# Down-projection weight loads of two rows of 128 instead of four, and a double-buffered second layernorm, in an attention and BitLinear block on eight cores

## The chip, the cores and the metric

The kernel runs on the 8 NeuronCores of one Trainium2 chip. The batch of 16 sequences is split by sequence: each core takes 2, and the cores exchange nothing. The time is the device time in microseconds (us) of the slowest core. All numbers of the trace below are of core 3, the slowest in the profiled execution.

## The reference

One transformer layer with layernorm after each half. Shapes are x: (16, 2048, 1024), 16 heads of 64, INNER = 4096, all float32.

```python
x = _layernorm(x + attention(x, Wq, Wk, Wv, Wr))     # additive causal penalty, softmax
x = _layernorm(x + ffn(x))

def ffn(x, w_gate, w_up, w_down):      # _bitlinear: activations rounded to 8 bits per token,
    gate = silu(_bitlinear(x, w_gate)) # weights rounded to -1, 0, 1 times one scale
    up = _bitlinear(x, w_up)
    return _bitlinear(gate * up, w_down)
```

## The kernel before

The program is written out by hand: `Builder` appends every operation to a list for its engine (`Plan.add`), with the semaphore values it waits for, and each engine goes through its list strictly in order. Every DMA, loads, stores and DMA transposes alike, is issued by one engine, SyncE, from one list (`dma`, L135 to L144; `dmat` for transposes). So a DMA whose wait is not yet met holds back every DMA listed after it. `dmat` also waits until all DMAs issued so far have landed, and every later DMA waits until that transpose has landed (`dma_floor`).

For each of its two sequences a core computes attention in head pairs (`attn_pair`), then the output projection and the first layernorm (`wr_ln1`), which leaves the normalised rows in DRAM (`y1_sc`) and their 8-bit values transposed in SBUF (`XqT`), then the feed-forward part (`ffn`). The change touches only `ffn`.

`ffn` takes the 2048 tokens in four blocks (`tsb`) of 512 tokens, four tiles of 128 tokens each (`ti` 0 to 3):

- `phase_a(tsb)`: gate and up projection of the four tiles, 512 matmuls, with weights from `wgsb` and `wusb`.
- `quant(...)`: 8-bit rounding of the hidden rows on VectorE; `quant_tr` sends their transposition to `hqT`, one DMA transpose per tile. For tiles 0 and 1 it is issued at once, for tiles 2 and 3 later.
- `phase_b(tsb, half)`: down projection of two tiles (`half` 0: tiles 0 and 1; `half` 1: tiles 2 and 3). The contraction over INNER has 32 chunks of 128. They go in groups of WOC chunks; the weights of a group are one load (`load_b`) into one of the two halves of `wdsb`. A chunk is 4 matmuls (2 tiles by 2 column halves), into PSUM banks 4 to 7. The load for group `ow + 2` goes into the half that group `ow` used, and waits for the last matmul of group `ow`. With WOC = 4 there are 8 groups of 16 matmuls and 8 loads of 1 MB, 8 KB for each partition.
- The end of `phase_b`, in the text the epilogue: for each of the two tiles (`k` 0 and 1) a load of the residual from `y1_sc` into `z2`, two `stt` operations that add the scaled bank (they free the bank), ACT's Square with the sum of squares, eight small operations on single columns of `st`, a normalising `ts` in place, and a store of `z2` to `y_out`.

The order of the blocks is written in the last lines of `ffn`: half 1 of block `tsb - 1` is put off (`pend`) until after `phase_a` and `quant` of block `tsb`; then half 0 of block `tsb` follows. In that order each sequence has three put-off half 1 phases that come in the middle, four half 0 phases, and one last half 1 phase at the end. Before a put-off phase its first two loads are already there (`pre_b`, issued before `phase_a`). Before a half 0 phase the two first loads (`pre_b0`) are listed after the epilogue of the phase ahead, then the transposes of tiles 2 and 3, then the loads from the third on. The last phase has its first two loads listed directly before it.

In the kernel before there is one `z2` buffer. So the residual load for tile `k` = 1 waits for the store of tile `k` = 0 to land.

Of the kernel before, what the change touches and what calls it, by code (L numbers as in the profile page):

```python
# [8 lines left out]
F32 = mybir.dt.float32  # L9
BF16 = mybir.dt.bfloat16  # L10
AF = mybir.ActivationFunctionType
ALU = mybir.AluOpType
# [86 lines left out]
class Builder:  # L99
# [802 lines left out]
    def ffn(self, s, XqT, cg_cols, cu_cols):  # L902
        c = self.c
        S, D, DC, JT, INNER = c.S, c.D, c.DC, c.JT, c.INNER
        OC, OTILE, TSB = c.OC, c.OTILE, c.TSB
        HB = TSB // 2 or 1
        NH = TSB // HB
        WOC = 4
        with ExitStack() as _es:
            al = lambda *a, **k: _es.enter_context(self.sbg(*a, **k)).ap()  # L910
            htsb = al("htsb", [128, TSB * INNER], F32)
# [3 lines left out]
            wusb = al("wusb", [128, 2 * DC * 512], BF16)  # L915
            wdsb = al("wdsb", [128, 2 * WOC * D], BF16)
            gts = al("gts", [128, 2 * 512], F32)
            z2 = al("z2", [128, D], F32)
            cdc = al("cdc", [128, 2 * TSB], F32)
            st = al("stat2", [128, 16], F32)  # L920
            micol_d, t_mid = self.invsw["d"]

            state = dict(
                t_g_use=[None, None], t_u_use=[None, None],
                t_d_use=[None, None], t_y_use=[None],
                gts_user=[None, None],
                t_hq_free=[None, None],
                t_hqT_use=[None] * TSB,
                t_h_free=[None] * TSB,
                t_cd_use=[None] * (2 * TSB),  # L930
                prev_apply2=None, prev_y2_store=None, prev_ms2=None,
                prev_qtok=None)

            def load_a(ot):
# [110 lines left out]
            def load_b(ow):  # L1045
                b = ow % 2
                return self.dma(
                    wdsb[:, b * WOC * D:(b + 1) * WOC * D],
                    self.wT_sc["d"][:, ow * WOC * D:(ow + 1) * WOC * D],
                    waits=[state["t_d_use"][b]])  # L1050

            def phase_b(tsb, half, pre_ld=None):
                cdo = (tsb % 2) * TSB
                tis = range(half * HB, (half + 1) * HB)
                t_dn_grp = {ti: [None] * JT for ti in tis}
                t_hqT_tp = {ti: state["t_hqT_use"][ti] for ti in tis}
                for ow in range(OC // WOC):
                    b = ow % 2
                    if pre_ld is not None and ow < len(pre_ld):
                        t_ld = pre_ld[ow]  # L1060
                    else:
                        t_ld = load_b(ow)
                    for oi in range(WOC):
                        oc = ow * WOC + oi
                        for k, ti in enumerate(tis):
                            for jt in range(JT):
                                bk = 4 + k * JT + jt
                                w0 = [t_ld, t_hqT_tp[ti]]
                                if oc == 0:
                                    w0.append(self.bank_user[bk])  # L1070
                                lastmm = (k == HB - 1 and jt == JT - 1)
                                wmm = w0 if oc == 0 else (
                                    [t_ld] if (oi == 0 and k == 0 and jt == 0)
                                    else ())
                                t_dn_grp[ti][jt] = self.mm(
                                    self.bank[bk],
                                    hqT[:, ti * OC * 128 + oc * 128:
                                        ti * OC * 128 + oc * 128 + 128],
                                    wdsb[:, b * WOC * D + oi * D + jt * 512:
                                         b * WOC * D + oi * D + jt * 512 + 512],  # L1080
                                    oc == 0, oc == OC - 1,
                                    waits=wmm,
                                    force_inc=(lastmm and oi == WOC - 1))
                    state["t_d_use"][b] = t_dn_grp[tis[-1] if False else list(tis)[-1]][JT - 1]
                for k, ti in enumerate(tis):
                    state["t_hqT_use"][ti] = t_dn_grp[ti][JT - 1]
                    tc = tsb * TSB + ti
                    t_yl = self.dma(z2, self.y1_sc[:, tc * D:(tc + 1) * D],
                                    waits=[state["t_y_use"][0],
                                           state["prev_apply2"],  # L1090
                                           state["prev_y2_store"]])
                    t_zs = []
                    for jt in range(JT):
                        bk = 4 + k * JT + jt
                        t_z = self.stt(z2[:, jt * 512:(jt + 1) * 512],
                                       self.bank[bk],
                                       cdc[:, cdo + ti:cdo + ti + 1],
                                       z2[:, jt * 512: jt * 512 + 512],
                                       ALU.mult, ALU.add,
                                       accum_out=st[:, 4 + jt:5 + jt],  # L1100
                                       waits=[t_dn_grp[ti][jt], t_yl,
                                              state["t_cd_use"][cdo + ti],
                                              state["prev_apply2"]])
                        self.bank_user[bk] = t_z
                        t_zs.append(t_z)
                    state["t_y_use"][0] = t_zs[-1]
                    if JT > 1:
                        t_sum = self.tt(st[:, 6:7], st[:, 4:5], st[:, 5:6],
                                        ALU.add, waits=t_zs)
                    else:  # L1110
                        t_sum = self.copy(st[:, 6:7], st[:, 4:5], waits=t_zs)
                    t_sq = self.act(gts[:, 0:min(D, 1024)], z2, AF.Square,
                                    accum_out=st[:, 7:8],
                                    waits=t_zs + [state["prev_ms2"],
                                                  state["gts_user"][0],
                                                  state["gts_user"][1]])
                    state["gts_user"][0] = state["gts_user"][1] = t_sq
                    t_mean = self.ts(st[:, 8:9], st[:, 6:7], 1.0 / D, None,
                                     ALU.mult, waits=[t_sum])
                    t_ms = self.ts(st[:, 9:10], st[:, 7:8], 1.0 / D, None,  # L1120
                                   ALU.mult, waits=[t_sq])
                    state["prev_ms2"] = t_ms
                    t_m2 = self.ts(st[:, 10:11], st[:, 8:9], st[:, 8:9], None,
                                   ALU.mult, waits=[t_mean])
                    t_var = self.tt(st[:, 11:12], st[:, 9:10], st[:, 10:11],
                                    ALU.subtract, waits=[t_ms, t_m2])
                    t_sd = self.act(st[:, 12:13], st[:, 11:12], AF.Sqrt,
                                    bias=self.epsc, waits=[t_var])
                    t_rs = self.recip(st[:, 13:14], st[:, 12:13],
                                      waits=[t_sd, state["prev_apply2"]])  # L1130
                    t_lb = self.stt(st[:, 14:15], st[:, 8:9], -1.0,
                                    st[:, 13:14], ALU.mult, ALU.mult,
                                    waits=[t_rs, state["prev_apply2"]])
                    t_y2 = self.ts(z2, z2, st[:, 13:14], st[:, 14:15],
                                   ALU.mult, ALU.add, waits=[t_lb, t_sq])
                    state["prev_apply2"] = t_y2
                    state["prev_y2_store"] = self.dma(
                        self.y_out[s, tc * 128:(tc + 1) * 128, :], z2,
                        waits=[t_y2])

            pend = None
            pre = None
            for tsb in range(c.NTSB):
# [5 lines left out]
                if pend is not None:  # L1149
# [5 lines left out]
                       if tsb + 1 < c.NTSB else None)  # L1155
                pend = (tsb, 1)
            phase_b(*pend, pre_ld=[load_b(0), load_b(1)])

def _make_aux():
# [39 lines left out]
```

How the kernel before makes its waits and increments, by code:

```python
                def body(eng):  # L77
                    last = {}
                    for emit, waits, inc, tag in plans.ops[eng_name]:
                        for s, v in waits:
                            if last.get(s, -1) >= v:
                                continue
                            eng.wait_ge(plans.sems[s], v)
                            last[s] = v
                        try:
                            instr = emit(eng) if emit is not None else None
                        except Exception:
                            print(f"EMIT FAILED at {tag} on {eng_name}")
                            raise
                        if inc is not None:
                            s, k = inc
                            instr.then_inc(plans.sems[s], k)
```

## Time and profile before

| what | us |
|---|---|
| median of the 2 runs shown | 7968.22 |
| the two runs | 7871.26 and 8065.18 |
| the profiled execution's own time | 7871.26 |
| its span on core 3 | 7869.7 |
| spans of the other cores in it | 7811.2 to 7856.9 |

The profiled execution is the lower of the two runs. The page of the profile gives per engine the busy time and its share of the span, then the costliest groups of instructions by line of the kernel. Since every operation goes through a helper, a line names a helper (L160 is `mm`, L171 `act`, L193 `stt`, L143 `dma`), and what tells operations apart are the tiles: `wdsb,hqT` is the down projection, `z` is the tile `z2`. "Landing" is the time from the issue of a DMA to the moment its completion is seen. "Granted clock" is the share of TensorE's full clock that it was given.

### The profile page before, as it was taken

How to read it: one execution, taken by the hardware profiler on the slowest of the kernel's cores; microseconds unless marked ns; L12 is line 12 of the kernel's file. 1: busy time of each engine (PE TensorE's matmuls, PEld its weight loads, DVE VectorE, ACT ScalarE, POOL GpSimd, SP SyncE). 2: the span in 40 equal slices, each digit the busy share in tenths (PEclk: the TensorE clock that was granted, in tenths of full speed). 3: DMA queues.
4: the chain of work that ended last, by engine and by line, in shares of the span. 5: the costliest groups of instructions: out<-in, count | busy, mean ns of one | idle time of the engine just before them, and what ended most of it. 6: DMA issues, size and time to landing. Idle time of an engine off the chain costs nothing.

```text
span 7869.7 us, 55675 instructions; the slowest of 8 cores (7811.2 to 7869.7 us)
## 1 busy us (share of the span) xinstructions
PE 5225.1 (66%) x17938; PEld 1907.1 (24%) x17938; DVE 2866.3 (36%) x4730; ACT 1126.9 (14%) x2132; POOL 0.2 (0%) x4
## 2 busy tenths in 40 slices
PE   1677767767776547765733887788778845675675
PEld 0222222222221213322311222222222212232231
DVE  1545545545544223313321443344343422322221
ACT  0112112212112001110100221122112200110010
POOL 0000000000000000000000000000000000000000
PEclk9888888888877778887866898888888877887876
DMA  4324314224322234454442000000000022445444
GB/s 99 97 59 106 84 61 107 72 66 114 73 48 55 58 79 142 142 167 138 147 166 61 11 13 16 17 11 13 17 17 6 11 83 64 131 150 171 144 122 161
DMA packets 780411, 649.70 MB, mean 83 GB/s; under 512 B 515680, under 2 KB 712544, under 8 KB 763744
## 3 DMA queue, kind: packets, MB, share of 16 engines
q1 hardware_dynamic: 780128, 646.15, 29.2%
q8 instruction: 150, 2.46, 0.1%
q14 instruction: 133, 1.09, 0.0%
HBM read 469.89 MB, written 75.50 MB: 69 GB/s over the span
## 4 chain that ended last, share of the span: by engine, by line
PE 53%; DVE 18%; DMA 17%; issue 6%; ACT 5%; SPq 1%; DVEq 0%; ACTq 0%
PE bank L160 52%; DMA wdsb<-wdT_sc 4%; ACT abuf L171 3%; DVE rls L209 3%; DMA hqT<-hq 2%; DMA otl_b<-otl_sc 2%; DMA XT_lo<-xlo 1%; DMA XT_hi<-xhi 1%; DVE khp L198 1%; DVE klp L193 1%; DVE stat L204 1%; DVE khl L198 1%; DMA z<-y_sc 1%; DVE pacc L204 1%; DVE apwl L193 1%
## 5 line engine op out<-in xcount | busy, mean ns | idle before, releaser
L171 ACT ACTIVATE abuf<-bank,negC 128x512 f32<-128x512 f32 (+3 forms) x1664 | 832.9, 601 | 3297.2 <-DVE bank L188 2475.0
L160 PE MATMUL bank<-abuf,vp 128*65 128x512 f32 x2560 | 1272.4, 657 | 0.0
L160 PE MATMUL bank<-XT_hi,apwh 128*128 128x512 bf16 x1536 | 500.5, 492 | 853.6 <-DVE apwl L193 673.9
L160 PE MATMUL bank<-wdsb,hqT 128*128 128x512 bf16 x2048 | 529.9, 422 | 579.3 <-DMA wdsb<-wdT_sc 578.9
L160 PE MATMUL bank<-klp,khl 128*128 128x512 bf16 x1280 | 511.0, 399 | 336.9 <-ACT abuf L171 313.7
L209 DVE RECIPROCAL rls<-bank 1x512 f32<-1x512 f32 x128 | 429.5, 3355 | 732.7 <-PE bank L160 732.4
L160 PE MATMUL bank<-wgsb,XqT 128*128 128x512 bf16 x2048 | 508.8, 393 | 255.7 <-DMA wgsb<-wgT_sc 254.1
L160 PEld LDWEIGHTS bank<-abuf,vp 128*65 128x65 f32 x2560 | 379.2, 153 | 856.4 <-issue 855.4
L160 PE MATMUL bank<-qlo,khp 128*128 128x512 bf16 x1280 | 514.5, 402 | 0.0
L160 PE MATMUL bank<-wusb,XqT 128*128 128x512 bf16 x2048 | 501.6, 389 | 2.6 <-DMA wusb<-wuT_sc 2.6
L188 DVE TENSOR_TENSOR htsb<-bank,gts 128x512 f32<-128x512 f32 x256 | 177.1, 692 | 885.5 <-PE bank L160 757.2
L160 PEld LDWEIGHTS bank<-XT_hi,apwh 128*128 128x128 bf16 x1536 | 178.3, 120 | 1180.7 <-issue 1113.6
L160 PE MATMUL bank<-wrh,oth_b 128*128 128x512 bf16 x512 | 181.5, 532 | 420.6 <-DMA otl_b<-otl_sc 353.0
L160 PEld LDWEIGHTS bank<-wdsb,hqT 128*128 128x128 bf16 x2048 | 212.0, 106 | 896.2 <-issue 748.0
L160 PE MATMUL bank<-XT_hi,apwl 128*128 128x512 bf16 x1536 | 349.3, 381 | 0.0
L160 PE MATMUL bank<-XT_lo,apwh 128*128 128x512 bf16 x1536 | 348.7, 380 | 0.0
L160 PEld LDWEIGHTS bank<-wgsb,XqT 128*128 128x128 bf16 x2048 | 205.0, 100 | 517.3 <-issue 313.9
L160 PEld LDWEIGHTS bank<-klp,khl 128*128 128x128 bf16 x1280 | 125.8, 98 | 819.6 <-issue 794.6
L193 DVE SCALAR_TENSOR_TENSOR z<-bank,cdc,z 128x512 f32<-128x512 f32 x64 | 45.5, 749 | 744.3 <-PE bank L160 621.1
L171 ACT ACTIVATE gts<-bank,cg_cols 128x512 f32<-128x512 f32 x256 | 176.0, 687 | 709.8 <-PE bank L160 709.7
L160 PEld LDWEIGHTS bank<-wusb,XqT 128*128 128x128 bf16 x2048 | 204.3, 100 | 260.0 <-issue 52.6
L188 DVE TENSOR_TENSOR bank<-bank,mask 128x128 f32<-128x128 f32 x512 | 139.9, 297 | 255.7 <-PE bank L160 250.9
(84 smaller groups left out, 3351.1 us busy)
## 6 DMA issues: line engine op xcount, KB each, us to landing
wdsb<-wdT_sc SPq DMA_DIRECT2D x128, 1024.0 KB, 5.3
wgsb<-wgT_sc SPq DMA_DIRECT2D x64, 1024.0 KB, 8.7
wusb<-wuT_sc SPq DMA_DIRECT2D x64, 1024.0 KB, 11.1
pw<-Wg SPq DMA_DIRECT2D x64, 512.0 KB, 4.6
pw<-Wu SPq DMA_DIRECT2D x64, 512.0 KB, 4.5
pw<-Wd SPq DMA_DIRECT2D x64, 512.0 KB, 4.9
x_tm<-x SPq DMA_DIRECT2D x2, 8192.0 KB, 27.3
xrd<-x SPq DMA_DIRECT2D x32, 512.0 KB, 5.2
```

The costliest lines, as they stand in the source:

```text
L160: e.matmul(o, l, r, start=a, stop=b),
L171: e.activation(o, i, f, bias=b, scale=s, accum_out=a),
L188: e.tensor_tensor(o, a, b, p), waits, ("dve", 1))
L193: e.scalar_tensor_tensor(o, a, s, b, p0, p1, accum_out=ac),
L198: lambda e, o=out_ap, i=in_ap: e.tensor_copy(o, i),
L204: e.tensor_reduce(o, i, AX, p, apply_absolute_value=a),
L209: lambda e, o=out_ap, i=in_ap: e.reciprocal(o, i),
```

## The change

It does two things, both in `ffn`.

1. WOC goes from 4 to 2. `wdsb` halves (16 KB to 8 KB for each partition). A `phase_b` has 16 groups of 8 matmuls and 16 loads of 512 KB (4 KB for each partition) in place of 8 groups of 16 and 8 loads of 1 MB. There are still two buffers, and `pre_b`, `pre_b0` and the loads of the last phase are still two loads. Matmuls and bytes in sum stay as they are.
2. The epilogue gets two `z2` buffers and two sets of columns in `st`, used in turn (`par`), and a scratch tile `sqb` for Square's output in place of `gts`. A buffer's residual load waits for Square, the normalising operation and the store of the tile two before. The waits on `prev_apply2`, `prev_y2_store`, `prev_ms2`, `t_y_use` and `gts_user` go from the epilogue. The order of the lists stays: load 0, operations of tile 0, store 0, load 1, operations of tile 1, store 1.

```diff
-        WOC = 4
+        WOC = 2
...
-            z2 = al("z2", [128, D], F32)
+            z2 = [al("z2a", [128, D], F32), al("z2b", [128, D], F32)]
+            sqb = al("sqb", [128, D], F32)
...
-                    t_yl = self.dma(z2, self.y1_sc[:, tc * D:(tc + 1) * D],
-                                    waits=[state["t_y_use"][0],
-                                           state["prev_apply2"],
-                                           state["prev_y2_store"]])
+                    par = state["ep_i"] % 2
+                    state["ep_i"] += 1
+                    po = 12 * par
+                    z2p = z2[par]
+                    sqp = sqb
+                    t_yl = self.dma(z2p, self.y1_sc[:, tc * D:(tc + 1) * D],
+                                    waits=state["z2_users"][par])
...
-                    t_sq = self.act(gts[:, 0:min(D, 1024)], z2, AF.Square,
-                                    accum_out=st[:, 7:8],
-                                    waits=t_zs + [state["prev_ms2"],
-                                                  state["gts_user"][0],
-                                                  state["gts_user"][1]])
-                    state["gts_user"][0] = state["gts_user"][1] = t_sq
+                    t_sq = self.act(sqp, z2p, AF.Square,
+                                    accum_out=st[:, 7 + po:8 + po],
+                                    waits=t_zs)
...
-                    state["prev_apply2"] = t_y2
-                    state["prev_y2_store"] = self.dma(
-                        self.y_out[s, tc * 128:(tc + 1) * 128, :], z2,
+                    t_st = self.dma(
+                        self.y_out[s, tc * 128:(tc + 1) * 128, :], z2p,
                         waits=[t_y2])
+                    state["z2_users"][par] = [t_sq, t_y2, t_st]
```

## Rows read from the trace of the kernel before

**Rows 1.** The page: busy time of each engine, share of the span, instructions.

```profile
PE 5225.1 (66%) x17938; PEld 1907.1 (24%) x17938; DVE 2866.3 (36%) x4730; ACT 1126.9 (14%) x2132; POOL 0.2 (0%) x4
```

**Rows 2.** The page, chain that ended last: shares of the span by engine.

```profile
PE 53%; DVE 18%; DMA 17%; issue 6%; ACT 5%; SPq 1%; DVEq 0%; ACTq 0%
```

**Rows 3.** Waits: engine, line, what for, us in total, times, longest.

```profile
PE bank L160 <- DMA wdsb<-wdT_sc: 578.9, 75, 33.3
...
DVE z L193 <- DMA z<-y_sc: 123.2, 16, 9.2
```

**Rows 4.** Chain that ended last, 7674 to 7707 us: start, duration, piece.

```profile
7674.23 4.56 DMA wdsb<-wdT_sc
7678.80 0.14 issue
7678.93 5.54 PE bank L160 x16
7684.54 4.72 DMA wdsb<-wdT_sc
```

**Rows 5.** The same chain, from the put-off phase's epilogue to the next phase.

```profile
7714.04 2.75 DMA y<-z
7716.92 3.40 DMA z<-y_sc
...
7725.89 0.34 SPq L143
7726.37 0.32 SPq L143
7726.85 7.30 DMA wdsb<-wdT_sc
...
7747.98 4.73 DMA wdsb<-wdT_sc
```

**Rows 6.** The same chain: first and last second-tile epilogue of the second sequence.

```profile
6935.20 3.23 DMA y<-z
6938.55 5.11 DMA z<-y_sc
...
7801.73 6.65 DMA wdsb<-wdT_sc
...
7853.94 3.08 DMA y<-z
7857.16 3.47 DMA z<-y_sc
```

**Rows 7.** Stretches (us, busy PE, PEld, DVE, ACT, POOL, granted clock, DMA share, GB/s): four half 0 phases.

```profile
6898.03:6928.54 30.51, 22.91 (x95) 9.51 (x96) 0.00 (x0) 0.00 (x0) 0.00 (x0) 0.85 0.60 224
...
sum 130.61, PE 98.89 PEld 39.58 DVE 0.00 ACT 0.00 POOL 0.00; mean PE 24.72 PEld 9.90 DVE 0.00 ACT 0.00 POOL 0.00
```

**Rows 8.** Stretches: sum of the three put-off phases; then the last phase.

```profile
sum 96.40, PE 73.04 PEld 29.47 DVE 37.88 ACT 0.00 POOL 0.00; mean PE 24.35 PEld 9.82 DVE 12.63 ACT 0.00 POOL 0.00
...
7801.73:7848.60 46.87, 36.13 (x128) 13.93 (x128) 0.07 (x1) 0.00 (x0) 0.00 (x0) 0.73 0.56 202
```

**Rows 9.** The page, DMA issues: number, KB each, median us to landing.

```profile
z<-y_sc SPq DMA_DIRECT2D x32, 512.0 KB, 5.5
y<-z SPq DMA_DIRECT2D x32, 512.0 KB, 3.0
```

**Rows 10.** Landing of all loads of `wdsb`, then `pw`, then `wstage`.

```profile
DMA to landing us min/median/max: 4.5/5.3/15.4
...
DMA to landing us min/median/max: 3.6/4.7/8.7
...
DMA to landing us min/median/max: 3.4/4.2/8.2
```

**Rows 11.** PE in order of time: start, duration, what, count [idle before, releaser].

```profile
7689.40 8.56 PE L160 MATMUL bank<-wdsb,hqT 128*128 128x512 bf16 x32 [0.74 <-DMA wdsb<-wdT_sc]
...
7732.00 3.57 PE L160 MATMUL bank<-wdsb,hqT 128*128 128x512 bf16 x8 [23.92 <-DMA wdsb<-wdT_sc]
```

More of the change, by code:

```diff
@@ L917, in ffn @@
             gts = al("gts", [128, 2 * 512], F32)
-            z2 = al("z2", [128, D], F32)
+            z2 = [al("z2a", [128, D], F32), al("z2b", [128, D], F32)]
+            sqb = al("sqb", [128, D], F32)
             cdc = al("cdc", [128, 2 * TSB], F32)
-            st = al("stat2", [128, 16], F32)
+            st = al("stat2", [128, 28], F32)
             micol_d, t_mid = self.invsw["d"]
@@ L924, in ffn @@
                 t_g_use=[None, None], t_u_use=[None, None],
-                t_d_use=[None, None], t_y_use=[None],
+                t_d_use=[None, None], ep_i=0,
                 gts_user=[None, None],
@@ L930, in ffn @@
                 t_cd_use=[None] * (2 * TSB),
-                prev_apply2=None, prev_y2_store=None, prev_ms2=None,
+                z2_users=[[], []],
                 prev_qtok=None)
@@ L1094, in phase_b @@
                         bk = 4 + k * JT + jt
-                        t_z = self.stt(z2[:, jt * 512:(jt + 1) * 512],
+                        t_z = self.stt(z2p[:, jt * 512:(jt + 1) * 512],
                                        self.bank[bk],
                                        cdc[:, cdo + ti:cdo + ti + 1],
-                                       z2[:, jt * 512: jt * 512 + 512],
+                                       z2p[:, jt * 512: jt * 512 + 512],
                                        ALU.mult, ALU.add,
-                                       accum_out=st[:, 4 + jt:5 + jt],
+                                       accum_out=st[:, 4 + po + jt:
+                                                    5 + po + jt],
@@ L1101, in phase_b @@
                                        waits=[t_dn_grp[ti][jt], t_yl,
-                                              state["t_cd_use"][cdo + ti],
-                                              state["prev_apply2"]])
+                                              state["t_cd_use"][cdo + ti]])
                         self.bank_user[bk] = t_z
                         t_zs.append(t_z)
-                    state["t_y_use"][0] = t_zs[-1]
                     if JT > 1:
-                        t_sum = self.tt(st[:, 6:7], st[:, 4:5], st[:, 5:6],
+                        t_sum = self.tt(st[:, 6 + po:7 + po],
+                                        st[:, 4 + po:5 + po],
+                                        st[:, 5 + po:6 + po],
@@ L1109, in phase_b @@
                                         ALU.add, waits=t_zs)
                     else:
-                        t_sum = self.copy(st[:, 6:7], st[:, 4:5], waits=t_zs)
-                    t_sq = self.act(gts[:, 0:min(D, 1024)], z2, AF.Square,
-                                    accum_out=st[:, 7:8],
-                                    waits=t_zs + [state["prev_ms2"],
-                                                  state["gts_user"][0],
-                                                  state["gts_user"][1]])
@@ L1117, in phase_b @@
-                    state["gts_user"][0] = state["gts_user"][1] = t_sq
-                    t_mean = self.ts(st[:, 8:9], st[:, 6:7], 1.0 / D, None,
+                        t_sum = self.copy(st[:, 6 + po:7 + po],
+                                          st[:, 4 + po:5 + po], waits=t_zs)
+                    t_sq = self.act(sqp, z2p, AF.Square,
+                                    accum_out=st[:, 7 + po:8 + po],
+                                    waits=t_zs)
+                    t_mean = self.ts(st[:, 8 + po:9 + po],
+                                     st[:, 6 + po:7 + po], 1.0 / D, None,
@@ L1119, in phase_b @@
                                      ALU.mult, waits=[t_sum])
-                    t_ms = self.ts(st[:, 9:10], st[:, 7:8], 1.0 / D, None,
+                    t_ms = self.ts(st[:, 9 + po:10 + po],
+                                   st[:, 7 + po:8 + po], 1.0 / D, None,
                                    ALU.mult, waits=[t_sq])
-                    state["prev_ms2"] = t_ms
-                    t_m2 = self.ts(st[:, 10:11], st[:, 8:9], st[:, 8:9], None,
+                    t_m2 = self.ts(st[:, 10 + po:11 + po],
+                                   st[:, 8 + po:9 + po],
+                                   st[:, 8 + po:9 + po], None,
@@ L1124, in phase_b @@
                                    ALU.mult, waits=[t_mean])
-                    t_var = self.tt(st[:, 11:12], st[:, 9:10], st[:, 10:11],
+                    t_var = self.tt(st[:, 11 + po:12 + po],
+                                    st[:, 9 + po:10 + po],
+                                    st[:, 10 + po:11 + po],
                                     ALU.subtract, waits=[t_ms, t_m2])
-                    t_sd = self.act(st[:, 12:13], st[:, 11:12], AF.Sqrt,
+                    t_sd = self.act(st[:, 12 + po:13 + po],
+                                    st[:, 11 + po:12 + po], AF.Sqrt,
@@ L1128, in phase_b @@
                                     bias=self.epsc, waits=[t_var])
[L1129 to L1134, printed above, removed]
+                    t_rs = self.recip(st[:, 13 + po:14 + po],
+                                      st[:, 12 + po:13 + po], waits=[t_sd])
@@ L1135, in phase_b @@
+                    t_lb = self.stt(st[:, 14 + po:15 + po],
+                                    st[:, 8 + po:9 + po], -1.0,
+                                    st[:, 13 + po:14 + po],
+                                    ALU.mult, ALU.mult, waits=[t_rs])
+                    t_y2 = self.ts(z2p, z2p, st[:, 13 + po:14 + po],
+                                   st[:, 14 + po:15 + po],
                                    ALU.mult, ALU.add, waits=[t_lb, t_sq])
-                    state["prev_apply2"] = t_y2
```

## The prediction

> **What bounds the kernel now.** I read the page first: TensorE (PE) is busy for 66% of the span and no other engine for more than 36% [rows 1]. The chain that ended last gives 53% to PE and 17% to DMA [rows 2], so there is DMA time on the path that sets the end, and the change can only matter there. The waits say where. PE waited 578.9 us for loads of `wdsb`, and VectorE (DVE) 123.2 us, 16 times, for the residual load of `z2` [rows 3]. Sixteen is the number of `phase_b` calls (2 sequences by 8): one wait in each epilogue, that of tile `k` = 1. The change touches both waits.
>
> The chain in order of time shows the first of them closely [rows 4]. In a `phase_b` PE runs 16 matmuls, then a load of `wdsb` is issued, 4.72 us later it has landed, and only then does PE go on. The reader should see load and matmuls alternate on the chain: a load is not hidden. The reason is in the code. With two buffers, the load for group `ow + 2` is issued when group `ow` ends, and all that covers it is the matmuls of group `ow + 1`. So two groups take L + G + 0.2 us, where L is a load's landing, G the time of one group's matmuls, and 0.2 the two hand-overs (0.14 after a landing and about 0.06 before an issue [rows 4]). This holds as long as L is longer than G.
>
> G comes from the stretches. From the landing of the transposes to the last matmul, the four half 0 phases of the second sequence take 130.61 us with 98.89 us of PE busy, the three put-off ones 96.40 with 73.04 [rows 7, 8]. Each holds 6 groups, so G = (98.89 + 73.04) / 42 = 4.1 us. L has a minimum of 4.5 and a median of 5.3 over all loads [rows 10]; I use 5.0 for the steady part of a phase, between the 4.72 of [rows 4] and that median. The model then gives, for the six groups of such a stretch, 4.7 (first load) + 0.14 + 2 x 4.1 + 2 x (5.0 + 4.1 + 0.2) = 31.6 us. Measured are 130.61 / 4 = 32.7 and 96.40 / 3 = 32.1. It is good to 3%, so I trust its form.
>
> **The change, part by part: smaller loads.** The same bytes now go in 16 loads of 512 KB, and a group is 8 matmuls, G' = 4.1 / 2 = 2.05 us. What decides is L', the landing of a 512 KB load. If landing were proportional to size, nothing would change. It is not. Two loads of 1 MB issued together are both there after some 7.8 us (7726.37 to 7734.15), where one alone takes 4.5 to 4.7 [rows 5, 10]; the second megabyte adds only about 3. Taking half of that off a minimum of 4.5 gives 3.0 to 3.2. Other loads of exactly 512 KB say more: `pw` never lands before 3.6 us and has a median of 4.7, `wstage` 3.4 and 4.2 [rows 10]. The nearest row is the residual load, 4 KB for each partition from a DRAM tensor with the same row pitch of 64 KB as the down weights. Alone in the queue, as in the second tile of an epilogue, it took 3.40 to about 5.3 us, on average 4.3 over the eight of the second sequence, of which the first and the last took 5.11 and 3.47 [rows 5, 6]. The lower bound is 3.0, what the median store takes [rows 9] and what the halved increment gives; the upper bound 4.7, no gain from the smaller size. I take 3.8: the floor of 3.4 plus the 0.4 to 0.5 by which the 1 MB load's steady value lies over its own floor.
>
> The Trainium skill, "DMA: Bandwidth & Descriptors", section "Anatomy of one DMA", fits a DMA as about 2.0 us fixed plus its bytes at 436 GB/s, and its rules for kernel authors ask for 1 MiB or more in one DMA. By it a 1 MB load takes 4.4 us, which the trace bears out with 4.5, and a 512 KB load 3.2 (an estimate from that fit); the residual loads here take more. With 3.2 the sum below would come out 68 us lower, at about 7923.
>
> Two groups now take 3.8 + 2.05 + 0.2 = 6.05 us, so what were two groups before takes 12.1 us in place of 9.3.
>
> - *Half 0 phases (8 in all).* After the transposes 14 groups remain in place of 6, because the two preloaded groups are half as big: 3.8 + 0.14 + 2 x 2.05 + 6 x 6.05 = 44.3 us, against 32.7: +11.6. Ahead of the transposes something is won: `pre_b0` needs 7.30 us to land, and the transposes wait for that [rows 5]. With half the bytes I take 2.5 us off. Net +9.1, times 8 = +73 us.
> - *Put-off phases (6).* 44.3 against 32.1: +12.2, times 6 = +73. The preloading in front of `phase_a` is hidden either way.
> - *Last phases (2).* 46.87 us before [rows 8]. After: 4.2 for the first load (6.65 before, two being issued together [rows 6]) + 0.14 + 4.1 + 7 x 6.05 = 50.8: +3.9, times 2 = +8.
>
> Sum: +154 us. It depends on L' with 7 loads in 14 phases and 8 in two, 114 in all: 11.4 us for each 0.1 us of L'.
>
> **The epilogue.** The residual load of the second tile waited for the store of the first to land: 2.75 us, then 3.40 us for the load, then the `stt` operations [rows 5]. In the second sequence the eight stores took 3.16 us on average, the first and last 3.23 and 3.08 [rows 6]. With two buffers the load goes out behind the store's issue, 0.48 us later (two issues in a row start 0.48 apart [rows 5]). The list order still keeps it behind the store, and the store behind the normalising operation of tile 0, so no more than the landing is won: 3.2 + 0.1 - 0.5 = 2.8 us. The load now shares the 16 DMA engines with the store's 512 KB; half of the 3 us that a further megabyte costs is 1.5 us if all of it falls into the load and nothing if the store is through. I take 0.6, so 2.2 us an epilogue. All of it is on the path, since everything that comes next (`pre_b0`, the loads of `phase_a`, the end of the sequence) is listed behind the second store. 16 x 2.2 = -35 us; the bounds are 16 x 1.3 = -21 and 16 x 2.8 = -45. The residual load of tile 0 was covered by a load (about 4.7) and a group (4.1) and now by 3.8 + 2.05 + 0.14 = 6.0 us, while its median landing over all 32 is 5.5 [rows 9]: just covered, and if the cover is gone it costs up to 1 us in each phase, +16 us. The other edits cost nothing: Square writes elsewhere but takes its place in ACT's list as before, ACT idles there, and the dropped waits had been met by earlier work of the same engine. The eight more loads and semaphore increments in a phase cost SyncE's queue 0.32 us each [rows 5], and it stands idle between loads.
>
> **Sum.** +154 - 35 = +119 us. Against the profiled execution's 7871 us that is 7990 us, 1.5% more. The median of the two runs shown, 7968, lies between the profiled run and one 2.5% above it; I reckon from the profiled one.
>
> **The rivals.**
>
> 1. *The small load lands no faster than the residual load does* (L' of 4.3 or more). For it speak the residual rows, the median of `pw`, and that the number of rows in a transfer (128) does not change; against it that the floors of all 512 KB loads are near 3.5. At 4.3: 119 + 57 = +176, 8047 us; at 4.7: +222, 8093. This is slower by over 2% from L' = 4.15 on.
> 2. *The clock falls.* PE would idle 1.95 of 6.05 us, about a third, where it now idles about a quarter of the stretch, at a granted clock of 0.73 to 0.87 [rows 7, 8]. Should it sink to 1.2 GHz, the lower of its two levels, a group of 8 would take the 3.57 us that 8 matmuls need after a wait of 23.92 us today [rows 11], and two groups 3.8 + 3.57 + 0.2 = 7.57: 1.52 more, 98 times (6 pairs in 14 phases, 7 in two), and 2 x 1.52 more at the head of 16 phases: 149 + 49 = +198 us on top, 8188. It decides (over 2% slower) once a fifth of these groups run so. Against it speaks that 32 matmuls after a gap of 0.74 us take 8.56 us [rows 11], 2.14 for 8 of them, so a short gap leaves the clock up; one of 2 us no row shows.
> 3. *The epilogue wins and the loads cost little* (L' of 3.0 or less, as for stores): 119 - 91 = +28 at 3.0, and at 2.6 -18 with a full 2.8 us an epilogue making it about -28, 7843 us: a shade faster. Break-even is at L' = 2.75. Against it: no 512 KB load of the trace landed under 3.4 in any of the rows read.
> 4. *The load size does not matter at all*, because a phase is bound by what stands ahead of it (transposes, quantisation). Then only the epilogue counts: -35, 7836 us. The alternating chain of rows 4 speaks against it.
>
> **How the numbers follow.** My forecast (L' from 3.3 to 4.15, +60 to +157) has 0.57. Rival 1 has 0.20, rival 2 has 0.08, rival 3 has 0.11, rival 4 has 0.04. The time of the likeliest is 7990 us; the range goes from 7900 (L' = 3.0) to 8110 (L' = 4.7 and a little less from the epilogue), which leaves out rivals 2 and 4 and the ends of 1 and 3. About 2% is what a measurement of this kernel can tell from no change. Over 2% slower starts at 8029 us: rivals 1 and 2 and the upper edge of the forecast, 0.32. Over 2% faster is not reached by any sum here, 0.03. The rest is 0.65.
>
> **What would show it.** In the profile after: `wdsb` landings of 512 KB with a median near 4 and a steady value near 3.8; PE's wait for `wdsb` up by about 150 us from 578.9; on the chain, 8 matmuls of about 2 us alternating with loads; the half 0 and put-off stretches at 44 us; VectorE's 16 waits for `z2`'s load shorter, and the second load's issue half a microsecond behind the store's. I am wrong if these stretches stay near 32 us, if `wdsb` lands in under 3.2 us, or if the granted clock in them drops well under 0.7.

## The result and the profile after

| | before | after |
|---|---|---|
| median of all executions, us | 8028.95 (12) | 8210.1 (13) |
| lowest, us | 7829.57 | 7993.72 |
| the profiled execution, us | 7871.26 | 7993.72 |
| ratio after to before | | 1.0202, 95% interval 1.0161 to 1.0243 |

The two medians mix in executions in which one die (four cores) or both were granted a lower clock; the ratio leaves these out, and so do the cores read below and the "quiet dies", those with a granted clock of 0.82 or more, each taken with the median time of its four cores. The 13 quiet dies of the kernel after lie at 7965 to 7985 us, median 7971; those of the kernel before, 46 over all the runs of this case, at 7801 to 7848, median 7814. So the change makes the kernel about 2% slower, some 156 us.

The profiled execution came out at 7993.72 us, where 7990 was forecast. That is luck: the forecast added too little to a base that was too high, as the part on the prediction shows. The median of 8210 lies outside the forecast range of 7900 to 8110.

First the waits of the kernel after (engine, line, what for, us, times, longest), to be held against [rows 3]:

```profile
PE bank L160 <- DMA wdsb<-wdT_sc: 744.5, 216, 32.8
...
DVE z2a L193 <- DMA z2a<-y_sc: 328.0, 6, 73.5
...
DVE z2b L193 <- DMA z2b<-y_sc: 94.1, 16, 7.7
```

PE waits for `wdsb` 216 times, not 75, and 165.6 us longer in sum. In both kernels 24 of these waits are the long ones in front of a phase and behind the transposes, 10.5 us or more each: 521 us of the 578.9 before and 530 of the 744.5 after. The short ones inside the stretches went from 59 us to 214: that is where the change costs. The second tile's wait for its residual load has fallen from 123.2 to 94.1 us, no more. The 328.0 us against `z2a` need care. They are the whole idle time of VectorE in front of six operations whose last releaser was the load; most of it is the phase itself. In only one of the 16 phases did the first `stt` start after the last matmul's end, by 0.97 us.

The DMA issues of the page after (number, KB each, median us to landing), against [rows 9, 10]:

```profile
wdsb<-wdT_sc SPq DMA_DIRECT2D x256, 512.0 KB, 3.7
```

Half the bytes land in 3.7 us where all of them took 5.3. The chain that ended last, in a put-off phase of the kernel after (start, duration, piece), answers to [rows 4, 5]:

```profile
7465.92 4.19 DMA wdsb<-wdT_sc
7470.11 0.14 issue
7470.25 5.12 PE bank L160 x16
...
7475.43 4.32 DMA wdsb<-wdT_sc
...
7479.89 1.90 PE bank L160 x8
...
7481.85 3.40 DMA wdsb<-wdT_sc
...
7485.39 1.90 PE bank L160 x8
...
7499.29 3.55 DMA wdsb<-wdT_sc
...
7502.98 1.90 PE bank L160 x8
...
7505.47 5.91 DMA z2a<-y_sc
...
7518.10 0.34 SPq L143
...
7518.58 4.51 DMA z2b<-y_sc
```

From 7475.43 to 7505.0 there are five turns of load and 8 matmuls, 5.9 us each: four such half-size groups in 11.8 us, where two groups of 16 took 9.3 on average in the half 0 and put-off phases of the kernel before. The last two lines show the new epilogue: the second residual load starts 0.48 us behind the first store's issue, as forecast, but still 0.48 us behind, and not beside the first tile's work.

The stretches from the first load after the transposes to the last matmul (us, busy PE, PEld, DVE, ACT, POOL, granted clock, DMA share, GB/s) sum over all half 0 phases of both sequences, eight of them, as follows. First the kernel before:

```profile
sum 268.50, PE 198.46 PEld 78.65 DVE 3.50 ACT 0.00 POOL 0.00; mean PE 24.81 PEld 9.83 DVE 0.44 ACT 0.00 POOL 0.00
```

And the kernel after, with the first of its eight rows:

```profile
3115.20:3160.90 45.70, 28.71 (x112) 10.58 (x112) 0.28 (x1) 0.00 (x0) 0.00 (x0) 0.90 0.56 173
...
sum 370.80, PE 233.15 PEld 85.61 DVE 3.25 ACT 0.00 POOL 0.00; mean PE 29.14 PEld 10.70 DVE 0.41 ACT 0.00 POOL 0.00
```

That is 33.6 us a phase before and 46.4 after; a stretch holds 112 matmuls in place of 96, and PE idles for 17.2 us of it in place of 8.8. The granted clock in it is 0.90, above the 0.85 of [rows 7].

### The profile page after: what moved, and what is told of

Same layout as the page of the kernel before. It is cut to its first block, busy times and chain, and to the rows that moved or that the text cites. A ratio compares the mean times of both kernels' runs of the same rounds, so it can differ in the third digit from the quotient of the medians.

```text
span 7992.2 us, 56145 instructions; the slowest of 8 cores (7952.8 to 7992.2 us)
## 1 busy us (share of the span) xinstructions
PE 5215.4 (65%) x17938; PEld 1891.2 (24%) x17938; DVE 2866.8 (36%) x4730; ACT 1127.7 (14%) x2132; POOL 0.2 (0%) x4
## 4 chain that ended last, share of the span: by engine, by line
PE 52%; DMA 18%; DVE 18%; issue 6%; ACT 4%; SPq 1%; DVEq 0%; ACTq 0%
PE bank L160 51%; DMA wdsb<-wdT_sc 6%; DVE rls L209 3%; ACT abuf L171 3%; DMA otl_b<-otl_sc 2%; DMA hqT<-hq 2%; DMA XT_lo<-xlo 1%; DMA XT_hi<-xhi 1%; DVE khp L198 1%; DVE klp L193 1%; DVE stat L204 1%; DMA z2b<-y_sc 1%; DMA pterT<-pter 1%; DVE khl L198 1%; SPq L143 1%
## 5 line engine op out<-in xcount | busy, mean ns | idle before, releaser
L160 PE MATMUL bank<-wdsb,hqT 128*128 128x512 bf16 x2048 | 538.9, 414 | 744.7 <-DMA wdsb<-wdT_sc 744.5
L193 DVE SCALAR_TENSOR_TENSOR z2a<-bank,cdc,z2a 128x512 f32<-128x512 f32 x32 | 22.8, 749 | 812.9 <-PE bank L160 484.9
```

The source lines that it names most:

```text
L160: e.matmul(o, l, r, start=a, stop=b),
L193: e.scalar_tensor_tensor(o, a, s, b, p0, p1, accum_out=ac),
```

## The experiments

Theory: the loss is a load's landing that two buffers cover with one group only. Rivals: the new epilogue costs; small loads cost in themselves. In the expectations "the changed kernel" is the kernel after. Where a profile is of another core than the slowest, its number is given.

**The load size alone.**

```diff
 (kernel before)
-        WOC = 4
+        WOC = 2
```

> The kernel before with WOC = 2 and its old epilogue. Theory (the loss is the landing of a load that two buffers cover with one group only: two groups take L' + G' + 0.2 us): the stretches from the transposes to the last matmul take 45 to 46 us as in the changed kernel, PE's wait for wdsb is about 745 us, and the time is some 28 us over the changed kernel, 1.022 to 1.026 of the kernel before. Rival (the loss comes from the new epilogue, its scratch tile, its columns or the tighter cover of its first residual load): the time stays within 0.5% of the kernel before.

Measured: 1.0245 of the kernel before, interval 1.0156 to 1.0335. PE's wait for `wdsb` and the eight half 0 stretches:

```profile
PE bank L160 <- DMA wdsb<-wdT_sc: 759.2, 213, 32.0
```

```profile
sum 372.70, PE 231.46 PEld 85.46 DVE 3.90 ACT 0.00 POOL 0.00; mean PE 28.93 PEld 10.68 DVE 0.49 ACT 0.00 POOL 0.00
```

46.6 us a stretch, as in the kernel after. Six quiet dies lie at 7984 to 8009 us, median 7992, where 15 of the kernel before on the same chip lie at 7801 to 7835, median 7810. The whole loss, and more, comes from WOC.

**The epilogue alone.**

```diff
 (kernel after)
-        WOC = 2
+        WOC = 4
...
-            sqb = al("sqb", [128, D], F32)
...
-                    sqp = sqb
+                    sqp = gts[:, 0:min(D, 1024)]
...
-                                    waits=t_zs)
+                                    waits=t_zs + [state["gts_user"][0],
+                                                  state["gts_user"][1]])
+                    state["gts_user"][0] = state["gts_user"][1] = t_sq
```

> WOC = 4 as before, with the two z2 buffers and the two column sets; Square keeps writing into gts. Theory: the stretches stay at 33 us, the 16 epilogues get about 1.8 us shorter each, and the time is 25 to 35 us under the kernel before, 0.996. Rival (the epilogue is what costs): over the kernel before by 50 us or more.

Measured: 0.9957, interval 0.9911 to 1.0003. Its eight half 0 stretches:

```profile
sum 265.20, PE 191.38 PEld 77.07 DVE 3.42 ACT 0.00 POOL 0.00; mean PE 23.92 PEld 9.63 DVE 0.43 ACT 0.00 POOL 0.00
```

The stretches stay where they were. From the last matmul to the second store's issue the 16 epilogues sum to 271 us, against 297 in the kernel before and 296 with the load size alone; in the kernel after it is 269. The epilogue part wins 1.6 to 1.8 us each time. The interval still touches 1, but the quiet dies tell the two apart: 18 of this kernel lie at 7779 to 7810 us, median 7790, some 20 us under the 7810 of the kernel before and a little less than the 25 to 35 expected. The two parts multiply to 1.0245 x 0.9957 = 1.020, the ratio of the whole change.

**Four buffers of 512 KB.** As many bytes as `wdsb` had before, but a load goes out three groups ahead of its use. `pre_b`, too, becomes four loads.

```diff
 (kernel after, Square writing into gts as above)
         WOC = 2
+        NB = 4
...
-            wdsb = al("wdsb", [128, 2 * WOC * D], BF16)
+            wdsb = al("wdsb", [128, NB * WOC * D], BF16)
...
-                t_d_use=[None, None], ep_i=0,
+                t_d_use=[None] * NB, ep_i=0,
...
-                b = ow % 2
+                b = ow % NB
...
-                pre_b0 = [load_b(0), load_b(1)]
+                pre_b0 = [load_b(i) for i in range(4)]
...
-            phase_b(*pend, pre_ld=[load_b(0), load_b(1)])
+            phase_b(*pend, pre_ld=[load_b(i) for i in range(4)])
```

> The changed kernel's loads of 512 KB, but four buffers in place of two (as many bytes of wdsb as the kernel before had), four loads issued ahead; Square keeps writing into gts. Theory (a landing of 3.7 us costs only because one group of 1.9 us covers it): with three groups (5.7 us) as cover it is hidden, the stretches fall to what PE takes, 27 to 32 us, PE's wait for wdsb drops by over 300 us, and the time is 60 to 120 us under the kernel before, 0.985 to 0.992. Rival (smaller loads cost in themselves, by the bandwidth of 4 KB rows or by SyncE's issue of twice as many): the stretches stay over 40 us and the time over the kernel before.

> Four buffers of 512 KB with the new epilogue a second time, for an interval. Theory: 0.985 to 0.992 of the kernel before. Rival: 1.00 or more.

Measured: the lowest time is 7735.57 us, with 7820.91 as the kernel before's lowest on the same chip (0.989). Neither run gave an interval. The quiet dies lie at 7703 to 7718 us in the first run (six) and 7703 to 7713 in the second (five), medians 7712 and 7709, where the kernel before has 7810 and 7813 on the two chips: 0.987 both times. The eight half 0 stretches (core 5):

```profile
3104.40:3132.00 27.60, 23.04 (x96) 9.52 (x96) 0.47 (x1) 0.00 (x0) 0.00 (x0) 0.86 0.74 248
...
sum 231.10, PE 184.77 PEld 77.23 DVE 3.33 ACT 0.00 POOL 0.00; mean PE 23.10 PEld 9.65 DVE 0.42 ACT 0.00 POOL 0.00
```

28.9 us a stretch, with the same 512 KB loads; four groups being preloaded, it holds 96 matmuls as in the kernel before, which needed 33.6. That settles the rival: small loads with deeper cover are better than large loads with shallow cover. PE's wait for `wdsb` fell less than expected, from 744.5 us to 526.0 on core 5 (expected: by over 300), since 506 us of it are the 24 long waits, which stay. The short ones fell from 214 us to 20.

**Three buffers, two loads ahead of a phase.** The same edit with `NB = 3` and `pre_b`, `pre_b0` left at two loads.

> Loads of 512 KB with three buffers, two issued ahead of a phase; Square keeps writing into gts. Theory: a load is covered by two groups, 2 x 1.9 = 3.8 us, against a landing of 3.7 plus 0.2, so the alternation all but vanishes, three groups take about 5.9 us at most, and a stretch after the transposes takes 30 to 34 us against 46 in the changed kernel. Rival (each landing grows as more loads are in flight, so that buffers win nothing): stretches of 40 us or more.

Measured on core 5:

```profile
sum 301.60, PE 223.29 PEld 87.00 DVE 3.53 ACT 0.00 POOL 0.00; mean PE 27.91 PEld 10.87 DVE 0.44 ACT 0.00 POOL 0.00
```

37.7 us a stretch of 112 matmuls: between two and four buffers, but over the 30 to 34 expected. The three quiet dies lie at 7829 to 7849 us, 7840 in the median, against 7816 for the kernel before on that chip and 7971 for the kernel after. The miss is of the landing, which I took as fixed. It grows with the loads in flight: the landings (min, median, max) with two buffers, three (core 5) and four (core 5) are

```profile
DMA to landing us min/median/max: 3.4/3.7/13.7
```

```profile
DMA to landing us min/median/max: 3.5/4.8/12.4
```

```profile
DMA to landing us min/median/max: 3.4/5.4/13.7
```

With 4.8 a turn of three groups takes 4.8 + 1.9 + 0.2 = 6.9 us, and 14 groups 14 / 3 x 6.9 + 4.9 = 37.1, close to the 37.7. This sum was made after the run. With four buffers and 5.4 a turn of four groups takes 7.5 us, just what four groups of 1.9 take on PE.

**Loads of 256 KB.** The kernel after with `WOC = 1`.

> The changed kernel with WOC = 1: 32 loads of 256 KB a phase, two buffers, groups of 4 matmuls. Theory: two groups take L'' + G'' + 0.2; with G'' = 1.0 and L'' = 3.2 (0.9 us were saved from 1 MB to 512 KB, so 0.45 for the next halving) 4.4 us, a stretch after the transposes about 67 us, the time some 340 us over the changed kernel, about 8330. Rival (landing proportional to size from here): the time stays within 50 us of the changed kernel.

> WOC = 1 a second time, since all its cores showed a low granted clock in the first run. With the landings of the first run (median 2.6 us for 256 KB, against 3.7 for 512 KB and 5.3 for 1 MB) and groups of 4 matmuls at about 1.0 us, two groups take 3.8 us; a stretch after the transposes of 30 groups 57 to 60 us; the time 8200 to 8300 us.

Measured: 8605.89 us in the first run, with all cores at a granted clock of 0.77 to 0.79, and 8329.55 in the second at 0.81 to 0.82. The first run's half 0 stretches took 67.2 us each, just what was expected, but by two errors that cancel: the landing is 2.6 us, not 3.2, and PE takes 41 us of a stretch, not the 30 of 30 groups at 1.0. So the second expectation, with the right landing, missed with its 57 to 60 us. The rows of the second run are the eight half 0 stretches, the first of them ahead of the sum, and then PE in order of time in one half 0 phase (start, duration, what, count, idle before):

```profile
3106.10:3173.50 67.40, 42.65 (x120) 11.35 (x120) 0.31 (x1) 0.00 (x0) 0.00 (x0) 0.75 0.43 125
...
sum 557.90, PE 351.34 PEld 93.94 DVE 0.73 ACT 0.00 POOL 0.00; mean PE 43.92 PEld 11.74 DVE 0.09 ACT 0.00 POOL 0.00
```

```profile
7135.43 1.74 PE L160 MATMUL bank<-wdsb,hqT 128*128 128x512 bf16 x4 [0.61 <-DMA wdsb<-wdT_sc]
7137.66 1.02 PE L160 MATMUL bank<-wdsb,hqT 128*128 128x512 bf16 x4 [0.49 <-DMA wdsb<-wdT_sc]
7140.09 3.37 PE L160 MATMUL bank<-wdsb,hqT 128*128 128x512 bf16 x8 [1.41 <-DMA wdsb<-wdT_sc]
7144.61 1.02 PE L160 MATMUL bank<-wdsb,hqT 128*128 128x512 bf16 x4 [1.15 <-DMA wdsb<-wdT_sc]
```

69.7 us a stretch. Here the second rival of the prediction does appear. A group of 4 matmuls takes 1.02 us at best, but here one takes 1.74, and 8 take 3.37 where two groups at 1.02 take 2.04; the granted clock of the first stretch is 0.75. Behind the first 32 matmuls of each phase, 211 of the 384 groups took longer than 1.07 us, and 179 of 384 in the first run. PE is busy for 351 us in place of 233, though a stretch has only 120 matmuls in place of 112. In the kernel after, most groups of 8 take 1.89 us, but not all:

```profile
7489.23 1.89 PE L160 MATMUL bank<-wdsb,hqT 128*128 128x512 bf16 x8 [1.96 <-DMA wdsb<-wdT_sc]
7491.31 1.89 PE L160 MATMUL bank<-wdsb,hqT 128*128 128x512 bf16 x8 [0.20 <-DMA wdsb<-wdT_sc]
...
7584.79 5.45 PE L160 MATMUL bank<-wdsb,hqT 128*128 128x512 bf16 x16 [2.31 <-DMA wdsb<-wdT_sc]
...
7599.72 3.50 PE L160 MATMUL bank<-wdsb,hqT 128*128 128x512 bf16 x8 [3.72 <-DMA wdsb<-wdT_sc]
```

Behind the first 32 matmuls of each phase, 9 of its 192 groups took 2.06 to 3.57 us in place of 1.89. Five of the nine come after gaps of 1.96, 1.97, 2.31, 3.72 and 3.99 us, the other four right behind a slow group. Ten other gaps of over 1.9 us were followed by a group of 1.89.

**Both residual loads ahead of the first store**, in the kernel after.

```diff
+                yls = []
+                for k, ti in enumerate(tis):
+                    tc = tsb * TSB + ti
+                    par = (state["ep_i"] + k) % 2
+                    yls.append(self.dma(z2[par],
+                                        self.y1_sc[:, tc * D:(tc + 1) * D],
+                                        waits=state["z2_users"][par]))
                 for k, ti in enumerate(tis):
...
-                    t_yl = self.dma(z2p, self.y1_sc[:, tc * D:(tc + 1) * D],
-                                    waits=state["z2_users"][par])
+                    t_yl = yls[k]
```

> The changed kernel with both residual loads of an epilogue listed one after the other, ahead of the first tile's operations and its store. Theory (the second buffer wins little because the load still stands behind the store in SyncE's list, and behind the store's bytes): the second tile's first stt starts right behind the first tile's normalising operation instead of 5 to 7 us after the store's issue, each epilogue falls from 17 to about 11.5 us, and the time is 75 to 90 us under the changed kernel. Rival (something else holds the second tile, such as ACT's Square or the banks): no more than 20 us.

The chain in one epilogue:

```profile
7218.17 0.06 DVE z2a L182
...
7218.90 1.43 DVE z2b L193 x4
...
7223.29 0.82 DVE z2b L182
```

The second tile's `stt` now follows the first tile's last operation. The 16 epilogues sum to 172 us in place of 269, so 97 us are gone from them, 6 us each. The lowest time is 7938.42 us, 55 under the lowest of the kernel after, and the six quiet dies lie at 7889 to 7923 us, median 7899, 72 under the 7971 of the kernel after; 75 to 90 were expected. Part of the gain was lost in the stretches: on cores 3, 5 and 7 of the profiled execution the eight half 0 stretches sum to 405 to 407 us, with a landing median of 4.1, where the same cores have 371 to 379 in the kernel after; on cores 0, 1 and 6 they stand at 373 to 385 (after: 370 to 377). Why loads landed later on some cores stays open.

**Four buffers and early residual loads together.**

> Four buffers of 512 KB and both residual loads ahead of the first store. Theory: the two savings add, since they lie in different stretches: about 90 us from the shorter stretches plus 75 to 90 from the epilogues and the 28 that the second buffer gives, 0.975 to 0.982 of the kernel before.

Measured: 0.9792, interval 0.9734 to 0.985, and seven quiet dies at 7611 to 7673 us, median 7614, which is 202 under the kernel before. Four buffers alone gave 98 to 104, and the 16 epilogues sum to 174 us, 97 under the 271 with four buffers alone: the two savings add.

**The next phase's loads ahead of the stores.** On top of that, `phase_b` gets a `hook`, called between the residual loads and the epilogue's operations, which lists `pre_b0` and the transposes of tiles 2 and 3, or `load_a`, or the last phase's first loads.

```diff
+                hooked = hook() if hook is not None else None
                 for k, ti in enumerate(tis):
...
+                def hook_tr():
+                    ld = [load_b(i) for i in range(4)]
+                    quant_tr(tr23)
+                    return ld
+                def hook_a(tsb=tsb):
+                    if tsb + 1 < c.NTSB:
+                        return [load_a(0), load_a(1)]
+                    return [load_b(i) for i in range(4)]
+                pre_b0 = (phase_b(*pend, pre_ld=pre_b, hook=hook_tr)
+                          if pend is not None else hook_tr())
+                pre = phase_b(tsb, 0, pre_ld=pre_b0, hook=hook_a)
```

> As the one with four buffers and early residual loads, and in addition the next phase's first loads (and the transposes of tiles 2 and 3) are listed ahead of the epilogue's stores, so that they run beside the epilogue. Theory (the epilogue costs only because the list holds the next loads behind its stores): 6 transitions to a half 0 phase win about 8 us each, 6 to phase_a about 9, 2 to the last phase about 6, together some 110 us more, 0.960 to 0.970 of the kernel before. Rival (the next phase waits for its banks or for the transposes anyway): within 40 us of the version without this reordering.

> The reordered version a second time, for an interval: its lowest time so far is 7484.5 us beside 7825.7 us for the kernel before on the same chip. Theory: 0.955 to 0.970 of the kernel before. Rival (that run was a stray low one): 0.975 or more, no better than the version without the reordering at 0.979.

> The reordered version a third time, in five rounds against the kernel before, for the interval that the two earlier runs lacked (their lowest times, 7484.5 and 7478.5 us, against 7825.7 and 7890.9). Theory: 0.953 to 0.962 of the kernel before. Rival (the lowest times were strays): 0.97 or more.

Measured: lowest times 7484.50, 7478.50 and 7488.86 us, with 7825.71, 7890.94 and 7831.74 as the kernel before's: 0.956, 0.948 and 0.956. None of the three runs gave an interval, but six executions of this version lie under 7700 us (the lowest 7478, the highest of them 7685) and none of the kernel before under 7820. The 17 quiet dies lie at 7452 to 7502 us, with medians of 7464, 7462 and 7475 in the three runs, about 350 under the kernel before on the same chip (0.955 to 0.956) and 150 under the version without the reordering, where some 110 were expected. Its waits (third run, core 2) show where:

```profile
PE bank L160 <- DMA wdsb<-wdT_sc: 366.5, 54, 32.4
PE bank L160 <- DMA wgsb<-wgT_sc: 107.7, 8, 43.3
```

The wait for `wdsb` was 578.9 us in [rows 3], 526.0 with four buffers alone and 458.3 with the early residual loads as well; that for `wgsb`, the first load of `phase_a`, was 254.1 us in the kernel before and 205.4 without the reordering.

## Why the prediction was right in mechanism and wrong in its numbers

The sums by part, over both sequences (core 3, the profiled executions):

| part | forecast, us | measured, us |
|---|---|---|
| 8 half 0 stretches | +93 | 370.8 - 268.5 = +102 |
| 6 put-off stretches | +73 | 273.4 - 198.1 = +75 |
| 2 last phases | +8 | 109.8 - 90.6 = +19 |
| `pre_b0` landing earlier | -20 | -8 |
| 16 epilogues | -35 | 269 - 297 = -28 |
| sum | +119 | +160 |

- *The alternation* held, and so did the landing: 3.8 us forecast, a median of 3.7 measured, and 4.32, 3.40, 3.83, 3.79 and 3.55 us in the five turns of the chain shown, 3.78 on average. A group took 1.90 us, not 2.05. Over the 14 half 0 and put-off phases two groups took 6.02 us on average, forecast 6.05. The Trainium skill's fit ("DMA: Bandwidth & Descriptors", section "Anatomy of one DMA") gives 3.2 us for this size (an estimate from that fit). That section is about DMAs issued from GpSimd, which the prediction did not say; the loads here are issued by SyncE. The lowest of the 256 landings is 3.4; taking the page's figure would have made the miss larger.
- *The half 0 and put-off stretches* were right within 10%. What was mis-sized is their start. The first 16 matmuls behind the long wait took 5.12 us in the chain shown and 5.8 on average over the 14 stretches (the first 8 of them 3.3 to 3.6 us, in place of 1.9), where 4.1 stood in the sum. The prediction's G of 4.1 was an average that hid this: in the kernel before the first group of 16 behind the long wait took 5.1 to 6.6 us and most later ones 3.6.
- *The preloads* were the wrongly sized term. I took 2.5 us off for the halved `pre_b0`. From a put-off phase's second store to the first load after the transposes the kernel before took 22.4 us on average over six phases, the kernel after 21.4. The two loads are issued right behind the store. The second of them landed after 6.5 us on average, 5.8 to 7.4, where it had been 7.6: 1.1 us less for half the bytes.
- *The last phases* cost 19, not 8. In the second one the first load took 5.54 us, not 4.2, and later one load took 6.04 with a group pair of 6.57 behind it, in place of 3.8, at a lowered clock. The base of 46.87 us, too, was the longer of the two before: they took 43.4 and 47.2, and after 51.7 and 58.1. These are two phases, and I can't tell which part is chance.
- *The epilogues* gave 1.8 us each, forecast 2.2. The second residual load went out 2.6 us earlier, 0.49 us behind the store in place of 3.1, but landed in 5.2 us on average in place of 4.35: 0.8 us later for the store beside it, forecast 0.6.
- *The first residual load*, called just covered, was: it went out 5.0 to 5.4 us ahead of the last matmul's end in most phases and held up VectorE in one.
- *Rival 2*, the falling clock, hardly came with 8 matmuls a turn, in 9 groups of 192 where a fifth would have decided; the granted clock of the first stretch rose to 0.90. It came with 4 matmuls a turn. Rivals 3 and 4 fell with the stretches. Rival 1, a landing of 4.3 or more, fell with the landing, yet its result, over 2%, is about what came: the interval of 1.0161 to 1.0243 has the 2% inside it.

**The step that failed** is the base and the range laid around it: "I reckon from the profiled one", 7871 us. The median of all executions of the kernel before came out at 8029 us, 158 above that base, and the median of the kernel after at 8210, 100 above the range's upper end. What the range allowed on its base, +29 to +239, holds the measured change, +181 by the medians and +156 by the quiet dies. But it was built from the terms of the sum alone and made no room for what the two runs shown already told: the same kernel at 7871 and at 8065. Even from their median, 7968, it would have ended at 8207.

Against the lowest executions of the kernel before, near 7830, the profiled one was high: one of its eight `phase_a` took 136.5 us at a granted clock of 0.80, where the other seven took 112.6 to 115.5 and all eight of the kernel after 113, 27 us in sum. So an increment 40 us too small on a base 40 us too high gave 7990 beside a profiled 7994. The 40 us of the increment are the terms of the table that were mis-sized: the preloads by 12 us, the start of the stretches and their base by 11, the last phases by 11 and the epilogues by 7.

## What to carry to other kernels

When a load is released by the group that used its buffer, write down the turn: landing + one group + hand-over for every N buffers' worth of groups, or N groups if that is longer. Halving both the load and the group under two buffers makes the turn worse when the landing falls by less than half (here from 5.3 to 3.7 us in the median), and the same memory in four buffers of half the size made it better here (28.9 us against 33.6 for the same 96 matmuls, and 46.4 for 112 with two small buffers). More loads in flight land later, so take the landing at the depth that you plan. And reckon a forecast of a median from a median, with the spread of the executions in its range. A second buffer in an epilogue wins only what the order of the queue allows: here 1.8 us with the load still listed behind the store, 6 us more with it ahead, and most with the next phase's loads listed ahead of the stores.

## What the runs showed of the hardware

- The landing of a load of 128 rows: median 2.6 us for 256 KB, 3.7 for 512 KB and 5.3 for 1 MB, always with two buffers. With 512 KB and more loads in flight it is 4.8 (three buffers) and 5.4 (four).
- With groups of 8 matmuls and a gap before each (0.20 to 2.2 us in the phase shown) TensorE ran 183 of 192 groups in 1.89 us; the stretches stand at a granted clock of 0.82 to 0.93 with their slow start, most of them at 0.89 or more, where the busier ones before stood at 0.73 to 0.87. With groups of 4 and gaps of 0.4 to 1.5 us in the phase shown, about half the groups were slow (211 and 179 of 384 in the two runs), up to 8 matmuls in 3.4 to 3.5 us. The median gap is shorter, 0.8 us against 1.1, and yet the clock is lower. The runs do not tell which of the things that changed here (group, gap, the work of the other cores) does it.
- A store of 512 KB issued 0.49 us ahead of a load of 512 KB made that load land in 5.2 us on average, against 4.35 for the load alone.
